# Slot-table entries of 64 bytes in place of 8 bytes in a mixture-of-experts block on one core

## The reference, cut to what matters

```python
scores = softmax(x2d @ wg_router.T)
topk_w, topk_idx = top_k(scores, 6); topk_w /= sum(topk_w)
pos = cumsum(one_hot(flat_idx)) - 1          # place of each choice in its expert
valid = pos_in_e < C                         # C = 2 * (2048 * 6 // 32) = 768
xe = zeros(E, C, D).at[flat_idx, safe_pos].add(x_rep)
ye = (silu(xe @ w_gate) * (xe @ w_up)) @ w_down
y  = sum over the 6 choices of ye[flat_idx, safe_pos] * topk_w
out = x + attention branch + y + shared expert
```

## Time and profile before

| | |
|---|---|
| median of 3 runs | 944.23 us (942.65 to 945.47) |
| the profiled execution: span from its first to its last instruction | 978.4 us |
| what lies around that span | not given; the profiled execution's own time is 978.4 us or more |
| PE busy | 931.9 us, 95% of the span |
| DVE, ACT, POOL busy | 643.6, 517.0, 481.2 us |
| DMA | 189.0 MB, 193 GB/s in the mean |

### The profile page before, as it was taken

One profiled execution on the slowest core, in us unless ns is written; L12 is line 12 of the kernel. 1 busy time (PEld: TensorE's weight loads), 2 busy tenths in 40 slices (PEclk: granted clock), 3 DMA queues, 4 the chain that ended last, 5 costly groups with the idle time before them and its releaser, 6 DMA issues.

```text
span 978.4 us, 14013 instructions
## 1 busy us (share of the span) xinstructions
PE 931.9 (95%) x4564; PEld 825.2 (84%) x4564; DVE 643.6 (66%) x1102; ACT 517.0 (53%) x875; POOL 481.2 (49%) x349
## 2 busy tenths in 40 slices
PE   6999997998959699999999999999999999999997
PEld 5887885776838589999999999999999999998886
DVE  6879772454434387776776767766776776677674
ACT  6873540211103256656666566756666656666651
POOL 3000077545733226666566765665565564574321
PEclk9999999899959799999999999999999999999999
DMA  8551164121305679998899998998999999999764
GB/s 295 189 183 44 54 186 128 36 91 40 88 8 186 180 236 265 224 230 221 242 246 227 224 261 244 225 225 235 263 238 261 254 241 277 231 234 282 187 129 117
DMA packets 130858, 189.01 MB, mean 193 GB/s; under 512 B 19364, under 2 KB 76324, under 8 KB 130656
## 3 DMA queue, kind: packets, MB, share of 16 engines
q1 hardware_dynamic: 102864, 132.56, 43.3%
q0 software_dynamic: 26704, 55.01, 27.6%
q10 hardware_dynamic: 1216, 0.53, 0.2%
HBM read 119.59 MB, written 41.89 MB: 165 GB/s over the span
## 4 chain that ended last, share of the span: by engine, by line
PE 50%; DMA 11%; issue 8%; SPq 8%; DVE 7%; another core or an unknown queue 7%; POOL 5%; ACT 4%; ACTq 1%; DVEq 0%; POOLq 0%
PE p_gu L1164 9%; PE p_gu L1166 9%; PE p_gu L1165 9%; SPq L473 7%; DMA xnT<-xn_rows,ids 6%; PE p_y L1164 5%; PE p_y L1165 5%; PE p_y L1166 5%; DMA xnT<-xnT 3%; POOL xnT L704 3%; POOL out L718 2%; DMA xnT<-xn_rows 1%; PE p_gu L1270 1%; PE p_gu L1268 1%
## 5 line engine op out<-in xcount | busy, mean ns | idle before, releaser
L718 POOL DMA_INDIRECT out<-rows,ids x112 | 203.3, 1815 | 219.9 <-ACT rows L778 195.5
L1164 PE MATMUL p_gu<-xT_hi,w_hi 128*128 128x512 f32 (+12 forms) x816 | 289.2, 354 | 14.9 <-DVE xT_lo L1468 7.8
L1166 PE MATMUL p_gu<-xT_hi,w_lo 128*128 128x512 f32 (+12 forms) x816 | 289.6, 355 | 4.1 <-issue 4.1
L1165 PE MATMUL p_gu<-xT_lo,w_hi 128*128 128x512 f32 (+12 forms) x816 | 289.4, 355 | 3.0 <-issue 2.9
L704 POOL DMA_INDIRECT xnT<-xn_rows,ids x112 | 166.6, 1487 | 87.5 <-issue 33.3
L689 POOL DMA_INDIRECT slot_table<-pay,slot_i x96 | 101.2, 1054 | 160.3 <-DVE slot_i L1646 132.6
L1164 PEld LDWEIGHTS p_gu<-xT_hi,w_hi 128*128 128x128 f32 x816 | 154.7, 190 | 29.6 <-issue 9.9
L1165 PEld LDWEIGHTS p_gu<-xT_lo,w_hi 128*128 128x128 f32 x816 | 154.8, 190 | 18.5 <-issue 7.2
L1468 DVE TENSOR_TENSOR w_lo<-raw,w_hi 128x1024 fp32r<-128x1024 f32 (+2 forms) x140 | 168.5, 1205 | 2.7 <-issue 1.8
L1166 PEld LDWEIGHTS p_gu<-xT_hi,w_lo 128*128 128x128 f32 x816 | 154.7, 190 | 12.3 <-issue 4.5
L1164 PE MATMUL p_y<-w_hi,hT_hi 128*128 128x512 f32 (+1 forms) x368 | 147.0, 399 | 9.1 <-DVE hT_lo L1468 6.2
(11 more groups left out here) (196 smaller groups left out, 1133.5 us busy)
## 6 DMA issues: line engine op xcount, KB each, us to landing
raw<-L_ffn_w_gate SPq DMA_DIRECT2D x32, 704.0 KB
raw<-L_ffn_w_up SPq DMA_DIRECT2D x32, 704.0 KB
xnT<-xnT SPq DMA_DIRECT2D x424, 48.0 KB
raw<-L_ffn_w_down SPq DMA_DIRECT2D x32, 512.0 KB
raw<-L_ffn_w_down SPq DMA_DIRECT2D x32, 192.0 KB
xring<-out SPq DMA_DIRECT2D x20, 256.0 KB
out<-xring SPq DMA_DIRECT2D x20, 256.0 KB, 2.6
xnT<-xnT SPq DMA_DIRECT2D x80, 64.0 KB
```

What stands on the lines that cost most here:

```text
L718: pool.indirect_dma_start(out=out[:, :], in_=y_sb[t][0:n, :], in_offset=None, out_offset=bass.IndirectOffsetOnAxis(ap=ids[0:n, col:col + 1 ...
L1164: t_.matmul(dst, stat[0], mov[0], start=first, stop=False)
L1165: t_.matmul(dst, stat[0], mov[1], start=False, stop=False)
L1166: return t_.matmul(dst, stat[1], mov[0], start=False, stop=last)
```

## The change

Each entry of the table now takes 64 bytes (`ENTRY` = 16 words), of which the first two words count, and the scatter writes all 64: the source is a window of 16 words of `pay`, which begins at the entry and runs on into its neighbours. `pay` gets a tail of 8 pairs, set to zero. The prefill needs one tile of 16 partitions and writes 2 KB rows in four DMAs; the tile `h_sb` is no longer used for it. The load back brings 8 KB for each of 112 and 64 columns, in place of 1 KB, and so it goes into the halves of `xnT` of batches 3 and 2; the second of its DMAs waits until batch 2 was copied out (`s_xt`). The transposes read with a step of 16 words.

```diff
+ENTRY = 16
+PRE = S // ENTRY
-        tabrow = at("tabrow", [P, 2, 2 * P], F32, 2 * RAW + 4 * XT)
-        pay = sb("pay", [P, TOPK * TILES, 2])
+        pay = sb("pay", [P, TOPK * TILES + ENTRY // 2, 2])
+        entry = pay[:].rearrange("p n two -> p (n two)")
+        tabrow = [xnT[:, b].rearrange("p c (s w) -> p (c s) w", w=ENTRY) for b in (3, 2)]
-            tb = table[0:TABLE, :].rearrange("(b s) two -> b (s two)", s=P)
-            for i, tile in enumerate((sg, h_sb)):
-                g.memset(tile[0:COLS // 4, :], 0.0).then_inc(s_pool0, 1)
-                pool.wait_ge(s_pool0, 3 + 2 * i)
-                g.iota(tile[0:COLS // 4, 0::2], pattern=[[1, 2 * P]], base=T + 2 * P * i,
-                       channel_multiplier=0, allow_small_or_imprecise_dtypes=True).then_inc(s_pool0, 1)
-                pool.wait_ge(s_pool0, 4 + 2 * i)
-                for j in range(2):
-                    pool.dma_start(tb[2 * i + j::4, :], tile[0:COLS // 4, 2 * P * j:2 * P * (j + 1)]
-                                   ).then_inc(s_pre, 16)
+            tb = table[0:TABLE, :].rearrange("(b s) w -> b s w", s=P)
+            parts, groups = 4 * P // PRE, COLS // 4
+            by_part = table[0:TABLE, :].rearrange("(g p s) w -> p g (s w)", p=parts, s=PRE)
+            g.memset(sg[0:parts, :], 0.0).then_inc(s_pool0, 1)
+            pool.wait_ge(s_pool0, 3)
+            g.iota(sg[0:parts, 0::ENTRY], pattern=[[1, PRE]], base=T, channel_multiplier=PRE,
+                   allow_small_or_imprecise_dtypes=True).then_inc(s_pool0, 1)
+            pool.wait_ge(s_pool0, 4)
+            for i in range(4):
+                at_ = slice(groups // 4 * i, groups // 4 * (i + 1))
+                pool.dma_start(by_part[:, at_, :],
+                               sg[0:parts, :].unsqueeze(1).to_broadcast([parts, groups // 4, S])
+                               ).then_inc(s_pre, 16)
+            g.memset(pay[:, TOPK * TILES:, :], 0.0).then_inc(s_const, 1)
...
-                            out=table[:, :], in_=pay[:, c, :], in_offset=None,
+                            out=table[:, :], in_=entry[:, 2 * c:2 * c + ENTRY], in_offset=None,
...
-            pool.dma_start(tabrow[0:MAINB, 0, :], tb[0:MAINB, :]).then_inc(s_tabl, 16)
-            pool.dma_start(tabrow[0:XMAX, 1, :], tb[MAINB:COLS, :]).then_inc(s_tabl, 16)
+            pool.dma_start(tabrow[0][0:MAINB], tb[0:MAINB]).then_inc(s_tabl, 16)
+            pool.wait_ge(s_xt, TURNED)
+            pool.dma_start(tabrow[1][0:XMAX], tb[MAINB:COLS]).then_inc(s_tabl, 16)
...
-                    t_.transpose(p_tx[:, w * MAINB:(w + 1) * MAINB], tabrow[0:MAINB, 0, w::2],
+                    t_.transpose(p_tx[:, w * MAINB:(w + 1) * MAINB], tabrow[0][0:MAINB, :, w],
...
-                                        tabrow[0:XMAX, 1, w::2], ident[0:XMAX, 0:XMAX])
+                                        tabrow[1][0:XMAX, :, w], ident[0:XMAX, 0:XMAX])
...
-    table = nc.dram_tensor("slot_table", (TABLE + T * E, 2), F32, kind="Internal").ap()
+    table = nc.dram_tensor("slot_table", (TABLE + T * E, ENTRY), F32, kind="Internal").ap()
```

More of the change, by code:

```diff
@@ L671, in _ @@
             g.memset(before[:], 1.0).then_inc(s_const, 1)
-            pool.wait_ge(s_const, 6)
+            pool.wait_ge(s_const, 7)
             g.affine_select(out=before[:], in_=before[:], compare_op=ALU.is_gt, fill=0.0, base=0,
@@ L1554, in choices @@
             def choices():
-                dve.wait_ge(s_const, 7)
+                dve.wait_ge(s_const, 8)
                 for k in range(TOPK):
@@ L1565, in payload @@
                 link(v.reciprocal(r16[:, 5, :], r16[:, 4, :]))
-                by_ki = pay[:].rearrange("p (k i) two -> p k i two", k=TOPK)
+                by_ki = pay[:, 0:TOPK * TILES, :].rearrange("p (k i) two -> p k i two", k=TOPK)
                 v.tensor_copy(by_ki[:, :, :, 0], tok_id[:].unsqueeze(1).to_broadcast([P, TOPK, TILES]))
```

## The result

The changed kernel takes **952.86 us** (median of 4 runs, 951.41 to 956.5) where the kernel before takes 943.44 (median of 4, 940.62 to 945.47): ratio 1.0096, interval 1.007 to 1.0123, some **9 us slower**. The forecast was 945.7 us in a range of 939 to 952, so the median lies 0.9 us above the range. The side with 0.30 came, not the one with 0.53. The profiled execution is an ordinary one: its own time is 951.41 us, 1.8 us more than its span.

The account below looks back on a forecast made before the run. The prediction took PE's matmul stream as the bound from 340 to 940 us. It summed 944.2 + 1.0 (prefill) + 0.5 (load back) + 0 (scatter) + 0 (stalls) = 945.7 us, range 939 to 952.

Parts of the forecast that it names:

- The side with 0.30: Whole kernel: the chance given to a slower result; same had 0.53 and faster 0.17.
- Are they in the runs that are timed?: PE's stalls while POOL scatters, 34.3 us: claimed an effect of recording that timed runs lack, chance 0.85.
- Rival A: PE during the scatters: stalls are real, timed runs have them, wide entries end them; 911 us, chance 0.10.
- such windows: Profile after, 160 to 300 us: 90 matmuls per 20 us at full clock, if wide entries end the stalls.
- The scatter: POOL's 96 scatters into the table: issue time goes by entries, not bytes, so 0 us.
- The load back: Table's load before PE's first transpose: 3.3 us longer against 3.1 us of slack; 0.5 us taken, bounds 0 and 6.
- The reconstruction of POOL: POOL's scatter times shifted to a run without stalls: load issued at 265.3 us, table there at 268.0.
- Rival C: PE at the first transpose waits for a load sharing the engines with the second expert's weights; 950 us, chance 0.15.
- The prefill: Start of the kernel: 1.26 MB more at 368 GB/s, 3.4 us of work; 1.0 us taken, ends 0 and 3.4.
- a hole and cover behind: Behind the prefill: a 2 us DMA hole takes 1.9 us of the delay, existing waits cover part of the rest.
- The sum: Whole kernel: 944.2 + 1.0 (prefill) + 0.5 (load back) + 0 (scatter) + 0 (stalls) = 945.7 us.
- The later part: From 340 to 940 us: PE busy 598.6 of 600 us, the matmul stream bounds, the table change can't reach it.

Follow-up runs that it names:

- four groups: Follow-up sets of four kernels, each set on one chip; the kernel before took 970.28, 974.78, 944.75 and 943.64 us in them.
- before_third: The kernel before, unchanged, run and profiled again in the third set of follow-ups, on chip 11: 943.67 us (1 run).
- write_8_of_64: The changed kernel, but each scatter writes only 8 bytes into its 64-byte entry: 955.80 us, ratio 1.0111 to the kernel before.
- after: The changed kernel as first measured, unedited, against the kernel before: median 952.86 us, its profiled execution 951.41 us.
- after_c: The changed kernel, unedited, run again in the fourth set of follow-ups, on chip 13: 953.87 us, ratio 1.0100 to the kernel before.
- wide_source_c: The changed kernel with the prefill read from 64 partitions in place of 16: 953.88 us, ratio 1.0102 to the kernel before.
- both edits together: The changed kernel, prefill issued behind the last store of x, second expert's weights issued after the table landed; on chip 14: 970.03 us, ratio 0.9951.
- both_c: The changed kernel, prefill issued behind the last store of x, second expert's weights issued after the table landed; on chip 11: 944.48 us, ratio 1.0006.

## Why the prediction was wrong, point by point

**"Are they in the runs that are timed?"** gave a right number for a wrong reason, which is luck. The stalls are no effect of recording. In four groups a chip had them throughout or not at all: every profile of the first two groups shows them, for either kernel, and no execution of the kernel before there took less than 959 us, while none in the last two took more than 951. The profile before (span 978.4 us) was of that condition, the median of 944.23 us of the other. That the stalls filled the difference to 0.1 us was read as a difference between profiled and timed; it was one between two chips or two moments. Rival A (wider entries end real stalls, 911 us) fell, though it had the stalls right: they are real. The clean windows after belong to the condition of the chip, and not to the entries. The prediction had named such windows as a sign that wider entries end the stalls; that sign cannot tell the entries from the condition. The page that was quoted ("NOTIFIC — the notification-queue block" of the Trainium skill, section 7.1) says that the block holds back its producers when its inner pipeline is full; no run here shows that, and `before_third`, recorded in full with 8-byte writes, has no stall.

**The scatter** (0): right. 96 issues, 0.97 us for one, and `write_8_of_64` shows that the width neither costs nor gains. The 512-byte rule of the Trainium skill ("DMA: Bandwidth & Descriptors", Specifications) agrees so far: 8 and 64 bytes are on the same side of it and cost the same.

**The load back** (0.5, bounds 0 to 6): a step that failed, by 4.2 us, though inside its bounds. Each time was read off a profile with stalls and then shifted. "From issue to the second landing it took 2.7 us" was true only where the weights come 10 us behind the load; without stalls the same 176 KB take 7.2 us. The reconstruction of POOL put the load at 265.3 us, since it moved DVE's slots too little: it had those of choices 3 and 4 ready at 194.1 and 219.0, and `before_third` has them at 189.0 and 213.2. The load really goes at 258.6, in the same us as the weights, which had been placed well ("near 258"). So the slack was 1.5 us in place of 3.1, and the load took 13.7 us in place of 6.0. The 6.0, scaled from the zero stores, was too low even without the weights: alone the load took 8.3 us.

**Rival C** (0.15) is what happened, at its place and with its price of "4 to 6" for the load: 4.16 to 4.71 us of wait with the full 1.44 MB, 4.7 us by the ratios. Its condition, the weights "5 us later", was not needed: the load was 7 us earlier.

**The prefill** (1.0, bounds 0 to 3.4): mis-sized by 4.8 us, the most of all terms, and its upper bound too low. It is 5.8 us by the ratios and 4.9 to 8.1 us at the first scatter (129.13 to 132.31 against 124.19). The bound took 1.26 MB at the engines' 368 GB/s. The source on 16 partitions gives 101 GB/s at nearly full share, so the work is several times as long, and `W_out` shifts by 11 us (POOL goes on at 25.76 us, and at 14.97 in `before_third`) and not by up to 3.4. The prediction also looked for the cost at the loads of x alone. It stood earlier, at PE's eight transposes of `W_out`, which in `before_third` came without a wait:

```profile
20.44 1.12 PE L1160 MATMUL p_y<-ident,raw 128*128 128x128 f32 x8
```

They come at 25.52 and 25.77 us in the two profiles of the changed kernel, 5.1 and 5.3 us later. Behind them the first (`after`) goes on with a matmul every 0.23 us, the second (`after_c`) with one every 0.43 us until 32 us; its granted clock is 0.80 in the mean from 17 to 31 us. As far as these rows show, that is why its first scatter is 8.1 us late and not 4.9. And the other half of the argument, that a hole and cover behind swallow the delay, fails even with the wide source: the wait only moves on to the loads of x. A wait of PE there costs more than its length, too: in `wide_source_c` the clock is 0.94 from 30 to 60 us and 1.00 in `before_third`.

**The sum.** With the terms as measured, 5.8 for the prefill and 4.7 for the load, it is 944.2 + 10.5 = 954.7 us. The median is 952.86 here and 953.87 in `after_c`; rival C's 950 us lacks mainly the prefill.

**The later part** was right, nearly: the table doesn't reach it. The first matmul of unit 7 stands in the chain that ended last (start, us, what), in `before_third` and in the changed kernel:

```profile
295.33 0.74 PE p_gu L1164
```

```profile
305.34 0.74 PE p_gu L1175
```

From there to the end are 646.5 and 644.3 us. So the changed kernel comes to the experts 10.0 us later, and 2.2 us of that are given back behind it.

**Open.** What makes a chip stall PE was not found. That both edits together are under the kernel before on chip 14 (0.9951) and level with it on chip 11 goes with the fewer stalls of that run's profile; what made them fewer is open too. Without stalls no version here beats the kernel before, and `both_c` is level with it.

## What to carry to other kernels

Before a profile's rows are used against a median, see that both belong to one condition: here a span 34 us over the median meant another chip or another moment, and the order of events in it (weights 10 us behind the load) was not that of the timed runs. A transfer made eight times as large is priced by what is issued in the same us, and by how many partitions its source has, not by the engines' best rate; ask whether it could be issued where nobody waits, or whether one wait on a queue would keep it apart. Both costs here, 9 us together, went away with one transfer issued later and one wait added.

## What the runs showed of the hardware that was not expected

- Stalls of PE of 1.00 us and more, put down to "issue", came in all runs of a group or in none, on the same chip number (11: 970.28 us, later 944.75), in one stretch of the program (from some 160 to 300 us), with 8- and with 64-byte writes. The kernel before takes 26 to 31 us more with them.
- A prefill read from 8, 16 and 64 partitions ran at 53, 101 and 272 GB/s, and its packets took 0.83, 0.88 and 0.67 of the 16 engines' time: a full share is no sign of a full rate.
- 176 KB issued 0.7 us behind 2.1 MB of weights on another queue took 7.2 us, and 1.44 MB took 13.6 us in the same place and 8.3 with the weights behind it.
